# First SwiGLU under the second attention: silu of a token block in one piece, behind all eight first products

## The chip, the cores and the metric

The kernel runs on one core of one Trainium2 chip. The metric is the time of one execution in microseconds (us), as a median over runs; less is better. The engines are TensorE (PE, matmuls and transposes), VectorE (DVE), ScalarE (ACT, activations), GpSimd (POOL) and SyncE (SP, which issues DMAs).

## The reference, cut to what matters

Two transformer layers run over x of 2 batches x 1024 tokens x 256 channels. Layer 0 is windowed self-attention, a cross-attention that keeps the 16 best of 154 keys for each query and head, and a SwiGLU:

```
def _swiglu(h, w_m1, b_m1, w_m2, b_m2):
    u = h @ w_m1 + b_m1                  # 256 -> 2048
    a, b = (u[..., :HID], u[..., HID:])  # HID = 1024
    return jax.nn.silu(a) * b @ w_m2 + b_m2
```

Layer 1 is self-attention over all 1024 tokens, a masked cross-attention and an MLP with gelu. All is float32. Batch 1 still goes through layer 0 while batch 0 is already in layer 1.

## The kernel before, in words

The work of all engines follows one plan. `make_plan` gives every small step a due time by hand, and `Plan.finish` sorts the steps by it. Each engine's program then walks the one sorted list and emits its own part of each step, so that every engine runs its instructions strictly in the plan's order and waits on semaphores for the others. The plan has six stages of projections and MLPs (stage `s`, batch `b`, block `n` of 512 tokens) laid between the steps of four attentions.

The second attention is the one that keeps 16 keys (`topk_run`). A unit of it is one tile of 128 queries for two pairs of heads. Per unit, PE makes the scores of two halves (`c_scores`, L1162) into two of the banks 1 to 4. For each half DVE finds the 16 greatest (`c_top`, L1578 to L1588), ACT negates the maximum (`c_neg`, L1349) and takes the exponential (`c_exp_all`, L1359), and POOL masks it (`c_pick`, L1664 and L1666). PE turns both halves (`c_tail` and `c_turn`, L1173 and L1181) and ACT copies them (`c_copy`, L1370). The scores of a unit may overwrite a bank only when the exponential of the unit two before has read it. Every fourth unit is followed by the product with the values (`c_pv`, L1194 and L1196), a copy by ACT (`o_copy`, L1344) and a transpose (`o_turn`, L993).

Under this attention, two slots to a unit, lies the first SwiGLU for batch 0 (stage 3, `b` = 0, blocks 0 and 1), built by `gap_slots`. For a block, PE makes eight first products `ua` j = 0 to 7 (L1056; two matmuls of 128x512 in the program, four rows in the trace), each into bank 0 or 6, and ACT adds the bias and copies each to `hidden` (`ua_copy`, L1304), which frees the bank. Then come eight second products `ub` (also L1056), each multiplied by DVE with the silu of the first (`hid`, L1533), then the down projection (L1070). The silu runs on `hidden` in place, on ACT, in four instructions q = 0 to 3 of 128x1024 (two products j each, L1320). silu and exp stand in different activation tables: a silu after an exp, and an exp after a silu, is preceded by a table load (ACT_TABLE_LOAD). For batch 0 the plan puts q = 0, 1 behind the copy of j = 3 and q = 2, 3 behind that of j = 7. For batch 1 all four stand behind j = 7. The product `hid` j waits until silu q = j // 2 is done:

```
elif kind == "hid":
    dve.wait_ge(*g.ran("ub", s, b, n, j))
    dve.wait_ge(m.silu_done, plan.n("silu", s, b, n, j // 2) + 1)
```

Each place at which ACT goes over to silu and back is called a break below: block 0 has its first break at 323.2 us and its second at 337.8 us of the trace, block 1 at 429.8 us and 441.6 us.

Of the kernel before, what the change touches and what calls it, by code (L numbers as in the profile page):

```python
# [20 lines left out]
HT = HID // P  # L21
# [280 lines left out]
def gap_slots(s, b, n, apart=0):  # L302

    gap = [[]] * apart
    p0, p1 = 2 * n, 2 * n + 1
    if s in ATTENDED:
        rows = [] if s == 2 or (s, b) == (3, 0) or (s, b, n) == (3, 1, 0) else [("row", s, b, p0, 0), ("row", s, b, p1, 0)]
        head = [rows + [("on_turn", s, b, p0), ("on_copy", s, b, p0), ("on_turn", s, b, p1), ("on_copy", s, b, p1)],
                *gap, [("y_mm", s, b, p0), ("x_sum", s, b, p0), ("stats", s, b, p0)],
                [("y_mm", s, b, p1), ("x_sum", s, b, p1), ("stats", s, b, p1), ("rstd", s, b, n)], *gap]  # L310
    else:
        head = [[("stats", s, b, p0), ("stats", s, b, p1), ("rstd", s, b, n)], *gap]
    turns = [x for k in range(CK) for x in (("hat_turn", s, b, n, k), ("modulate", s, b, n, k))]
    head += [[("x_hat", s, b, p0), ("x_hat", s, b, p1)], *gap, turns]
    if s == 3:
        tail = gap + [[("ua", s, b, n, j), ("ua_copy", s, b, n, j)] for j in range(HT)]
        tail[apart + 2].append(("row", s, b, p0, 1))
        tail[apart + 6].append(("row", s, b, p1, 1))
        for j in ((HT - 1,) if b else (3, HT - 1)):
            tail[j + apart] += [("silu", s, b, n, q) for q in range(j // 4 * 2 * (1 - b), (j + 1) // 2)]  # L320
        tail += [[("ub", s, b, n, j), ("hid", s, b, n, j)] for j in range(HT)]
        for p in (p0, p1):
            tail += [[("down_part", s, b, p, 0)], [("down_part", s, b, p, 1)], [("down_part", s, b, p, 2)], [("down", s, b, p), ("out_sum", s, b, p)]]
        return head, tail
    tail = gap + [[("qk", s, b, n, u), ("qk_a" if s == 2 or u % 2 == 0 else "qk_d", s, b, n, u)] for u in range(UNITS[s])]
    if s in HAS_V:
        for t in (n * 4, n * 4 + 2):
            tail.append([("v", s, b, t), ("v_copy", s, b, t), ("v", s, b, t + 1), ("v_copy", s, b, t + 1)])
    return head, tail
# [188 lines left out]
def make_plan():  # L518
# [13 lines left out]
    plan.spread(mod, T + 0.4 * W, T + 2 * W)  # L532
    between = lambda first, last, per: [T + (c + (0.62 + i) / per) * R for c in range(first, last) for i in range(per)]
    plan.fill(joined([gap_slots(1, 1, n) for n in range(2)]), between(5, 15, 2), (0.2 * R, 0.3 * R))
    plan.at(T + 4.0 * W, ("load_w", "wa1"))
    plan.at(T + 18 * R, *[("row", 2, 0, p, 0) for p in range(4)], *[("row", 2, 1, p, 0) for p in range(4)], ("load_row", 2), ("load_row", 3))
# [8 lines left out]
    ctx.append([("load_vt",)])  # L545
    plan.spread(ctx, T + 3.6 * W, T + 5.2 * W)
    plan.fill(joined([gap_slots(2, 0, n, 1) for n in range(2)]), between(23, 33, 2), (0.2 * R, 0.3 * R))
    step = 5.2
    A2 = end + 3
# [8 lines left out]
    def under(first, last, slots, per, aside=0.3):  # L558
        return plan.fill(slots, [A2 + (first + (i + aside) / per) * step for i in range(int((last - first) * per))], (0.25 * step, 0.9 * step, 0.5 * step))

    under(1, 18, joined([gap_slots(2, 1, n) for n in range(2)]), 1)
    under(1, 7, late, 1, 0.8)
    plan.at(A2 + 8.5 * step, ("stash",), ("load_w", "m1"), ("load_w", "m2a"))
# [1318 lines left out]
```

## Time and profile before

| | before |
|---|---|
| median of 3 runs | 1472.02 us (1468.61 to 1472.67) |
| profiled execution, its own time | 1467.48 us |
| its span, first to last instruction | 1465.7 us |
| PE busy | 1359.6 us, 93% |
| DVE busy | 901.9 us, 62% |
| ACT busy | 726.0 us, 50% |
| POOL busy | 346.1 us, 24% |
| mean granted TensorE clock | 0.972 |

The profile is one execution. Its own time is 1.8 us over its span. A busy share is an average over stages that differ: what a change is worth is read where it lies. In rows of a timeline, the bracket at the end is the time the engine was idle before the row, and what released it.

### The profile page before, as it was taken

The page shows a single profiled execution, that of the slowest core. Times are in us where ns is not written, and L with a number is a line of the kernel's source. Part 1 is how long each engine was busy: PE and PEld are TensorE (multiplying, and loading weights), DVE is VectorE, ACT ScalarE, POOL GpSimd, SP SyncE. Part 2 cuts the span into 40 slices and gives each one's busy share as a digit, 9 for nine tenths or more (in the row PEclk, how much of TensorE's full clock was granted, in tenths as well). Part 3 has the DMA queues.
Part 4 walks back from the last instruction along what each step waited for, and adds up shares of the span by engine and source line. Part 5 has one row for each costly group of instructions (what it writes and reads, how often), then busy time and mean ns, then how long its engine had stood idle before and what let it go on. Part 6 is the DMA issues. An engine that isn't in the chain of part 4 may idle for free.

```text
span 1465.7 us, 25433 instructions
## 1 busy us (share of the span) xinstructions
PE 1359.6 (93%) x9100; PEld 681.3 (46%) x9100; DVE 901.9 (62%) x2785; ACT 726.0 (50%) x1484; POOL 346.1 (24%) x397
## 2 busy tenths in 40 slices
PE   7989887889999888999899999999999989989998
PEld 5457654444644653442233333343333335545676
DVE  3656579988888896765565666666676346640220
ACT  2245456665485564035544565555556664543221
POOL 1013257876666664010000100000010011010220
PEclk9999989889999999999999999999999999999999
DMA  6011003000000000000010000000000000000000
GB/s 196 21 56 34 17 19 107 2 15 1 1 2 12 30 2 28 1 1 1 1 52 21 1 2 0 2 1 1 1 12 1 2 1 2 13 6 0 15 19 29
DMA packets 22093, 26.75 MB, mean 18 GB/s; under 512 B 4204, under 2 KB 19634, under 8 KB 21708
## 3 DMA queue, kind: packets, MB, share of 16 engines
q1 hardware_dynamic: 21059, 25.03, 5.3%
q8 instruction: 73, 1.20, 0.3%
q14 instruction: 52, 0.43, 0.1%
q10 hardware_dynamic: 909, 0.10, 0.1%
HBM read 21.58 MB, written 3.08 MB: 17 GB/s over the span
## 4 chain that ended last, share of the span: by engine, by line
PE 78%; DVE 11%; ACT 4%; issue 4%; POOL 1%; DMA 1%; SPq 0%; ACTq 0%; DVEq 0%; POOLq 0%
PE bank L1098 27%; PE bank L1056 11%; PE bank L1138 8%; PE bank L1070 7%; PE bank L1035 5%; PE bank L1014 4%; PE bank L993 2%; PE bank L1162 2%; PE bank L1041 2%; DVE left L1581 2%; PE bank L1181 1%; DVE x_hat L1526 1%; DVE top L1578 1%; DVE left L1588 1%; PE bank L1021 1%
## 5 line engine op out<-in xcount | busy, mean ns | idle before, releaser
L1337 ACT ACTIVATE pr<-bank 128x512 f32<-128x512 f32 x656 | 353.4, 598 | 283.6 <-PE bank L1098 270.3
L1553 DVE TENSOR_REDUCE part_max<-bank 128x1 f32<-128x512 f32 x512 | 327.2, 685 | 178.5 <-PE bank L1098 178.0
L1098 PE MATMUL bank<-slot 32*128 32x512 f32 (+1 forms) x3072 | 388.2, 522 | 10.8 <-ACT pr L1337 6.1
L1098 PEld LDWEIGHTS bank<-slot 32*128 32x128 f32 x3072 | 162.6, 187 | 209.5 <-issue 157.8
L1605 POOL TENSOR_SCALAR var_eps<-mean_var 128x4 f32<-128x4 f32 x24 | 5.5, 229 | 882.5 <-DVE mean_var L1517 882.0
L1664 POOL TENSOR_SCALAR left<-left 128x308 f32<-128x308 f32 x128 | 125.3, 979 | 76.0 <-issue 34.3
L1138 PE MATMUL bank<-pr,v 128*17 128x512 f32 x1024 | 135.2, 600 | 0.2
L1056 PE MATMUL bank<-h_t,w_m 128*128 128x512 f32 x256 | 127.9, 625 | 4.3 <-DVE o_all L1497 3.2
L1666 POOL TENSOR_TENSOR probs<-left,exp_all 128x308 f32<-128x308 f32 x128 | 107.5, 840 | 10.7
L1359 ACT ACTIVATE exp_all<-bank,neg 128x154 f32<-128x154 f32 x256 | 85.6, 386 | 6.6 <-DVE left L1581 2.1
L1578 DVE MAX8 top<-bank 128x8 f32<-128x154 f32 x256 | 69.5, 313 | 30.6 <-PE bank L1162 30.0
L1557 DVE TENSOR_REDUCE neg_max<-bank 128x3 f32<-128x462 f32 (+1 forms) x96 | 50.7, 579 | 52.1 <-PE bank L1098 51.8
L1581 DVE MATCH_REPLACE8 left<-top,bank 128x154 f32<-128x154 f32 x256 | 76.8, 308 | 0.0
L1588 DVE MATCH_REPLACE8 left<-top,left 128x154 f32<-128x154 f32 x256 | 75.7, 303 | 0.3 <-issue 0.3
L1056 PEld LDWEIGHTS bank<-h_t,w_m 128*128 128x128 f32 x256 | 45.0, 195 | 64.2 <-issue 57.4
L1506 DVE TENSOR_TENSOR x_sb<-x_sb,bank 128x512 f32<-128x512 f32 x32 | 21.9, 684 | 83.6 <-PE bank L1014 83.6
L1344 ACT ACTIVATE o_st<-bank 128x512 f32<-128x512 f32 x64 | 38.3, 599 | 60.9 <-PE bank L1143 30.1
L1584 DVE MAX8 top<-left 128x8 f32<-128x154 f32 x256 | 68.1, 307 | 0.0
L1014 PE MATMUL bank<-w_out,o_norm_t 128*128 128x256 f32 x256 | 64.9, 398 | 1.4 <-DVE x_sb L1506 1.4
L1035 PE MATMUL bank<-h_t,wa 128*128 128x512 f32 x128 | 63.6, 625 | 2.7 <-ACT h_t L1270 2.0
L1636 POOL TENSOR_TENSOR x_sb<-x_sb,res_row 128x512 f32<-128x512 f32 x48 | 60.2, 1274 | 22.9 <-DMA res_row<-rows_dram 15.6
L1550 DVE TENSOR_REDUCE neg_max<-bank 128x4 f32<-128x512 f32 x64 | 40.9, 682 | 39.5 <-PE bank L1098 39.5
(142 smaller groups left out, 1757.0 us busy)
## 6 DMA issues: line engine op xcount, KB each, us to landing
w_m<-in_L_xcond_w_m SPq DMA_DIRECT2D x1, 2048.0 KB, 7.9
w_m<-in_L_xcond_w_m SPq DMA_DIRECT2D x2, 1024.0 KB, 7.9
w<-in_L_xcond_w SPq DMA_DIRECT2D x2, 1024.0 KB, 6.6
w_ada<-in_L_xcond_w_ada SPq DMA_DIRECT2D x1, 1792.0 KB, 10.1
x_sb<-in_x SPq DMA_DIRECT2D x6, 256.0 KB, 6.3
res_row<-rows_dram SPq DMA_DIRECT2D x12, 128.0 KB, 3.4
out_x<-x_sb SPq DMA_DIRECT2D x6, 256.0 KB, 2.1
wa<-in_L_xcond_w_qkv SPq DMA_DIRECT2D x1, 768.0 KB, 6.6
```

Of the source, the lines that this page charges most:

```text
L1014: last = nc.tensor.matmul(bank[:, tt * C:(tt + 1) * C], m.o_norm_t[:, slot, k, tt * P:(tt + 1) * P], m.w_out[:, j % 2, k, :], start=(k == ...
L1035: last = nc.tensor.matmul(bank[:, :], w[:, k, c0:c0 + P], m.h_t[:, slot, k, :], start=(k == 0), stop=(k == CK - 1))
L1056: last = nc.tensor.matmul(bank[:, :], w[:, k, c0:c0 + P], m.h_t[:, slot, k, :], start=(k == 0), stop=(k == CK - 1))
L1070: last = nc.tensor.matmul(bank[:, tt * C:(tt + 1) * C], m.hidden[:, j, t * P:(t + 1) * P], w, start=(j == 0), stop=(j == HT - 1))
L1098: last = nc.tensor.matmul(g.bank(*tile)[:, into], left, right, start=True, stop=True)
L1138: last = nc.tensor.matmul(out[h * HW:h * HW + VE, :], m.v[b][:, d % TB, heads[h], :], m.pr[:, slots[h], :], start=(d % TB == 0), stop=(d % ...
L1337: nc.scalar.activation(m.pr[:, u % NPR, :], g.bank("s", gi, i)[:, :], ACT.Exp).then_inc(g.free("s", gi, i), 1)
L1553: nc.vector.tensor_reduce(m.part_max[:, slot, h * TB + i // 8, i // 4 % 2:i // 4 % 2 + 1], bank[:, :], axis=AX.X, op=ALU.max).then_inc(don ...
L1581: nc.vector.match_replace(m.left1[:, v % 2, hh, :], m.top[:, v % 4, hh, 0:8], bank[:, hh * C:hh * C + S2], -FAR).then_inc(m.left1_done, 1)
L1588: nc.vector.match_replace(m.left2[:, v % 4, hh, :], m.top[:, v % 4, hh, 8:16], m.left1[:, v % 2, hh, :], -FAR).then_inc(m.left2_done, 1)
L1664: nc.gpsimd.tensor_scalar(left, left, -FAR, None, ALU.is_equal).then_inc(m.marked, 1)
L1666: nc.gpsimd.tensor_tensor(m.probs[:, u % 2, 2 * hf:2 * hf + 2, 0:S2], left, m.exp_all[:, v % 4, :, :], ALU.mult).then_inc(m.pick_done, 1)
```

## The change

For batch 0 the four silu instructions of a block stand together behind the copy of the eighth first product, as they did for batch 1 only.

```diff
@@ gap_slots, s == 3
         tail[apart + 6].append(("row", s, b, p1, 1))
-        for j in ((HT - 1,) if b else (3, HT - 1)):
-            tail[j + apart] += [("silu", s, b, n, q) for q in range(j // 4 * 2 * (1 - b), (j + 1) // 2)]
+        tail[HT - 1 + apart] += [("silu", s, b, n, q) for q in range(HT // 2)]
         tail += [[("ub", s, b, n, j), ("hid", s, b, n, j)] for j in range(HT)]
```

The steps of PE, DVE, POOL and SP come in the same order as before. Only ACT's order changes, at four places (two in each of the blocks 0 and 1 of batch 0). The change is one line shorter, so that lines behind it have numbers one lower.

ACT at the first break of block 0, before (L1304 the copies of products, L1320 silu, L1359 exp, L1344 the copy of the attention's values):

```order
L1304 ACTIVATE hidden<-bank,columns 128x512
L1320 ACT_TABLE_LOAD
L1320 ACTIVATE hidden<-hidden 128x1024 x2
L1349 ACTIVATE neg_74<-top 128x2
L1344 ACTIVATE o_st<-bank 128x512
L1359 ACT_TABLE_LOAD
L1359 ACTIVATE exp_all<-bank,neg_74 128x154 x2
L1304 ACTIVATE hidden<-bank,columns 128x512
```

The same place in the change:

```order
L1303 ACTIVATE hidden<-bank,columns 128x512
L1348 ACTIVATE neg_74<-top 128x2
L1343 ACTIVATE o_st<-bank 128x512
L1358 ACTIVATE exp_all<-bank,neg_74 128x154 x2
L1303 ACTIVATE hidden<-bank,columns 128x512
```

Two table loads and two silu instructions are gone from between the copies of the fourth and the fifth product.

ACT at the second break of block 0, before:

```order
L1304 ACTIVATE hidden<-bank,columns 128x512
L1320 ACT_TABLE_LOAD
L1320 ACTIVATE hidden<-hidden 128x1024 x2
L1349 ACTIVATE neg_74<-top 128x2
L1359 ACT_TABLE_LOAD
L1359 ACTIVATE exp_all<-bank,neg_74 128x154 x2
L1370 ACTIVATE probs_t<-bank 128x4x128
```

The same place in the change:

```order
L1303 ACTIVATE hidden<-bank,columns 128x512
L1319 ACT_TABLE_LOAD
L1319 ACTIVATE hidden<-hidden 128x1024 x4
L1348 ACTIVATE neg_74<-top 128x2
L1358 ACT_TABLE_LOAD
L1358 ACTIVATE exp_all<-bank,neg_74 128x154 x2
L1369 ACTIVATE probs_t<-bank 128x4x128
```

The two silu instructions stand here now, as four in a row between the same two table loads. In block 1 the same moves happen.

## Rows read from the trace of the kernel before

**Rows 1.** Page, busy time of each engine (share of the span) and instructions.

```profile
PE 1359.6 (93%) x9100; PEld 681.3 (46%) x9100; DVE 901.9 (62%) x2785; ACT 726.0 (50%) x1484; POOL 346.1 (24%) x397
```

**Rows 2.** Page, chain that ended last, shares of the span by engine.

```profile
PE 78%; DVE 11%; ACT 4%; issue 4%; POOL 1%; DMA 1%; SPq 0%; ACTq 0%; DVEq 0%; POOLq 0%
```

**Rows 3.** Stretches: length, busy of PE, PEld, DVE, ACT, POOL (count), PE clock, DMA.

```profile
343.00:387.00 44.00, 43.70 (x272) 25.87 (x272) 36.19 (x181) 18.95 (x61) 30.70 (x34) 1.00 0.01 2
...
430.00:447.00 17.00, 15.03 (x76) 6.58 (x75) 13.06 (x73) 16.35 (x30) 8.89 (x10) 1.00 0.08 24
```

**Rows 4.** Groups on ACT, forms apart: line, count, busy us, mean ns, idle before.

```profile
L1320 ACT ACTIVATE hidden<-hidden 128x1024 f32<-128x1024 f32 x16 | 15.8, 1046 | 0.1
...
L1320 ACT ACT_TABLE_LOAD x6 | 7.7, 1283 | 0.1
```

**Rows 5.** Timeline of ACT, block 0's first break: start us, length us, what.

```profile
326.53 0.57 ACT L1344 ACTIVATE o_st<-bank 128x512 f32<-128x512 f32 x1
...
328.42 0.67 ACT L1359 ACTIVATE exp_all<-bank,neg 128x154 f32<-128x154 f32 x2
328.98 0.69 ACT L1304 ACTIVATE hidden<-bank,columns 128x512 f32<-128x512 f32 x1
```

**Rows 6.** Timeline of ACT, second breaks: block 1 (first row), block 0 (the others).

```profile
440.84 0.69 ACT L1304 ACTIVATE hidden<-bank,columns 128x512 f32<-128x512 f32 x1 [0.33 <-PE bank L1056]
...
337.04 0.69 ACT L1304 ACTIVATE hidden<-bank,columns 128x512 f32<-128x512 f32 x1 [0.33 <-PE bank L1056]
...
339.04 2.00 ACT L1320 ACTIVATE hidden<-hidden 128x1024 f32<-128x1024 f32 x2
340.95 0.19 ACT L1349 ACTIVATE neg<-top 128x2 f32<-128x2 f32 x1
...
342.45 0.67 ACT L1359 ACTIVATE exp_all<-bank,neg 128x154 f32<-128x154 f32 x2
```

**Rows 7.** Timeline of PE around the four breaks.

```profile
328.10 0.60 PE L993 MATMUL bank<-ident,o_st 128*128 128x128 f32 x4
329.72 1.98 PE L1056 MATMUL bank<-h_t,w_m 128*128 128x512 f32 x4 [1.02 <-ACT hidden L1304]
...
343.27 0.79 PE L1162 MATMUL bank<-kc,slot 32*128 32x154 f32 x8 [0.96 <-ACT exp_all L1359]
...
345.90 0.42 PE L1173 MATMUL bank<-ident,probs 128*32 128x128 f32 x8
...
435.44 0.79 PE L1162 MATMUL bank<-kc,slot 32*128 32x154 f32 x8 [1.07 <-ACT exp_all L1359]
...
447.06 0.79 PE L1162 MATMUL bank<-kc,slot 32*128 32x154 f32 x8 [0.96 <-ACT exp_all L1359]
```

**Rows 8.** Timeline of POOL, the pick that the transposes at 345.90 need.

```profile
344.33 0.84 POOL L1666 TENSOR_TENSOR probs<-left,exp_all 128x308 f32<-128x308 f32 x1
```

**Rows 9.** Timeline of ACT, a batch 1 block with four silu in a row.

```profile
700.20 3.89 ACT L1320 ACTIVATE hidden<-hidden 128x1024 f32<-128x1024 f32 x4
704.11 1.28 ACT L1337 ACT_TABLE_LOAD   x1
```

**Rows 10.** Timeline of PE, first work behind two longer idle times elsewhere.

```profile
306.57 1.16 PE L1021 MATMUL bank<-ident,x_hat 128*128 128x128 f32 x8 [2.54 <-ACT x_hat L1312]
...
549.65 1.63 PE L1021 MATMUL bank<-ident,x_hat 128*128 128x128 f32 x8 [3.25 <-ACT x_hat L1312]
```

**Rows 11.** Stretches of 8 us behind idle times of PE: length, PE busy, PE clock.

```profile
86.83:94.83 8.00, 8.00 (x99) 1.00 0.01 2
...
306.57:314.57 8.00, 8.00 (x40) 0.58 0.01 2
...
549.65:557.65 8.00, 7.37 (x44) 0.79 0.00 1
572.35:580.35 8.00, 8.00 (x29) 1.00 0.00 0
...
343.27:351.27 8.00, 8.00 (x46) 1.00 0.01 2
```

## The prediction

> **What bounds the kernel now.** I read the page first: PE is busy for 93% of the span, ACT for half of it [rows 1], and the chain that ended last lies for 78% on PE and for 4% on ACT [rows 2]. So a piece of ACT work costs time only where PE stands still for it. I then read the stretches around the SwiGLU. In 343 to 387 PE is busy for 43.70 of 44.00 us and ACT for 18.95; in 430 to 447, which holds both breaks of block 1, ACT is busy for 16.35 of 17.00 us and PE for 15.03 [rows 3]. The work between the breaks is PE's, and at the breaks ACT is late. Last I read the timelines of ACT and PE at the four breaks. PE waits once behind each of them, for 1.02 and 0.96 us in block 0 and for 1.07 and 0.96 us in block 1, each time released by ACT [rows 7]. These four waits, 4.01 us together, are all that the present breaks cost, and they are what the change can touch.
>
> **The change part by part.** *Work removed.* Per block two table loads of 1.283 us go [rows 4], so ACT does 4 x 1.283 = 5.1 us less in all. The 16 silu instructions all remain. None of this counts by itself, since ACT is not the bound; what counts is when the copies and exponentials behind the breaks are done.
>
> *First breaks.* In block 0 the silu stand before the copy of the attention's values at 326.53, a table load, the exponential at 328.42 and the copy of the fifth product at 328.98 [rows 5]. PE has nothing more to do from 328.10 + 0.60 = 328.70 on and starts the sixth product at 329.72, in the bank that this copy frees [rows 7]. Without two table loads and 2.00 us of silu before it, some 4.6 us, the copy is done before 328.70 (it needs to come 1.0 us sooner), so the wait goes whole: -1.02. In block 1 the scores at 435.44 wait for an exponential, and that wait goes in the same way: -1.07. Sum -2.09 us.
>
> *Second breaks.* Here ACT arrives with nothing in arrear: it waited 0.33 us for PE before the copy of the eighth product, at 337.04 and at 440.84 [rows 6]. Since it was waiting for PE, the break starts as much sooner as PE does, and not more. The silu take longer: two take 2.00 us and end in the negation at 340.95, 1.91 us after their start [rows 6]; four in a row take from 700.20 to 704.11, 3.91 us [rows 9]. The difference is 2.00 us, and the exponential at 342.45, for which PE's scores at 343.27 wait [rows 6, 7], comes 2.00 us later against the break's start. PE has only the two second products and the transposes to do in between, as before, and had used these up 0.96 us before the exponential came. So the whole 2.00 us is idle time of PE, in each block: +4.00 us. The wait becomes 0.96 + 2.00 = about 2.96 us.
>
> *What is queued behind it.* On ACT the copy of the transposes and two more exponentials stand behind the longer break; all of them serve work that PE reaches only behind the late scores. The next transposes start at 345.90 and need the pick that POOL ends at 344.33 + 0.84 = 345.17 [rows 7, 8]. That pick waits for the same exponential as the scores, so both move by the same amount and the slack of 0.73 us stays. DVE multiplies the first second product when silu q = 0 is done, which is one silu behind the break's start, as soon as it wants it. I cost all of that at nothing. Nor does anything give the delay back: the 44 us behind are PE's own [rows 3]. DMAs, POOL's and SP's queues are not moved past.
>
> Sum without the clock: -2.09 + 4.00 = **+1.91 us**.
>
> *The clock.* The waits of about 1 us leave the granted clock alone: 1.00 over the 8 us from 343.27 on [rows 11]. The trace shows no wait of 2.96 us here, so I bound its price by the nearest rows, PE's idle times between 2.4 and 3.3 us. There are eight that begin at full clock. Behind two of them the clock stayed full, as at 86.83 and 572.35; behind three the mean over 8 us was 0.79 or 0.80, as at 549.65 (idle before it 3.25 us); behind three it was 0.56 to 0.58, as at 306.57 (idle before it 2.54 us) [rows 10, 11]. The clock then stood at its lower level, 1.2 GHz in place of 2.4, for part of the stretch. Time lost is 8 x (1 - clock), where PE is busy throughout: 0, 1.7 or 3.4 us. Behind the new waits PE is busy throughout, so this would be lost in full. Two waits with chances of 2, 3 and 3 in 8 give a sum of 0 (6%), 1.7 (19%), 3.4 (33%), 5.1 (28%) or 6.8 us (14%). I take **3.4 us**, the likeliest.
>
> The Trainium skill ("TensorE: Matmul & The Clock Gate", section "HAM oscillation — how this bites in real kernels") says that waits between pieces of matmul work can throttle the array anew each time, and asks for loops without them. It speaks against this change, which makes one longer wait from two short ones; the rows agree that long waits lower the clock, though not each one does. [...]
>
> **Forecast**: +1.91 + 3.4 = **+5.3 us**. The profiled execution took 1467.48 us, so the sum gives 1472.8 on it. The median shown, 1472.02, is 4.5 us above that execution, which is of the size of what one or two stretches of low clock are worth; on the median the forecast is **1477.3 us**. Some 0.3% of this kernel, 4.4 us, can be told from no change.
>
> **The rivals.**
> *The clock holds at both new waits.* The two idle times after which it did so [rows 11] speak for it, the other six against. Time +1.9, that is 1473.9 us.
>
> *The longer burst is absorbed.* If PE made up the 2.00 us later, because what it waits for later (a DVE sum or a copy) is not moved by the delay, only the gains stay: -2.1, that is 1469.9 us. Against it: the scores are made by PE, and DVE and POOL start from them, so that everything moves with PE.
>
> *ACT is the bound in the blocks, and the kernel gets faster.* At 96% busy in 430 to 447 [rows 3], ACT might set the pace there. Then a block shortens by the work removed, 2 x 1.283 = 2.57 us, two blocks by 5.1: 1466.9 us. This decides if ACT reaches the second break in arrear to PE, from that point on. The 0.33 us that it waited for PE there, in both blocks [rows 6], speak against it.
> The Trainium skill ("ScalarE: Activation LUTs", section "What ACT_TABLE_LOAD costs") adds a drain to each load and puts a switch at about 2.66 us. An estimate from that page gives 4 x 2.66 = 10.6 us saved on ACT, and this rival would lead to 1461.4 us. The trace disagrees: from the end of the negation, 340.95 + 0.19, to the exponential at 342.45 a switch takes 1.31 us [rows 6].
>
> *The change does not do what it says*: the order on ACT shows that it does. I give it nothing.
>
> **How the numbers follow.** The clock falls at one or both new waits, the forecast: 0.70, with times of 3.6 to 8.7 us over the median, 1475.6 to 1480.7. The clock holds: 0.13. Absorbed: 0.10. ACT the bound: 0.04. Something dearer, as a wait that grows behind the burst: 0.03. The range from **1470 to 1482 us** takes in the forecast's whole range, the case of a held clock and most of the absorbed one, and a us more on top for the spread of the runs. Slower by over 0.3% needs +4.4 us: that is the forecast except for its case of one short fall, some 0.53, and the dearer case: **0.55**. Within 0.3%: that one case, the held clock and the absorbed one: **0.39**. Faster by over 0.3%: **0.06**, ACT as bound and a lucky clock.
>
> **What would show it.** Right: ACT has four table loads fewer (two of L1319 in place of four for batch 0) and is busy some 5 us less; no wait of PE for ACT at the sixth product of block 0 nor at the scores behind the fourth product of block 1; one wait of 2.8 to 3.1 us before the scores at each second break, released by the exponential; up to two new stretches of low clock right behind them. The first step is wrong if PE still waits at the first breaks, the second if the waits at the second breaks are under 2.5 us or PE's idle time shrinks later by as much. The forecast as a whole is wrong if the waits are as said and the clock stays full behind both, or if lower clock elsewhere in the trace, at waits that the change does not touch, moves by more than this.

## The result and the profile after

The change makes the kernel 0.33% slower: the ratio to the kernel before is 1.0033, with a 95% interval of 1.0021 to 1.0046, that is 4.9 us (3.1 to 6.8) on 1470. The median is 1474.18 us over 20 runs, that of the kernel before 1469.98 us, also over 20 runs; these medians lie 4.2 us apart, which is inside the interval. The three runs known ahead lay 2 us higher. One of the 20 runs of the change was disturbed (2166.39 us at a mean clock of 0.555) and is left out of the ratio and of all that follows; the median without it is 1474.07 us.

| | after |
|---|---|
| median | 1474.18 us |
| profiled execution, its own time | 1470.45 us |
| its span | 1468.7 us |
| mean granted TensorE clock | 0.974 |

The profiled execution is the third fastest of the 20, and only 3.0 us slower than that of the kernel before.

The page of the change, busy time of each engine, against [rows 1]:

```profile
PE 1358.5 (92%) x9100; PEld 680.2 (46%) x9100; DVE 901.3 (61%) x2785; ACT 721.3 (49%) x1480; POOL 346.0 (24%) x397
```

ACT has four instructions fewer and is busy 4.7 us less, and the kernel is slower all the same. The groups of ACT say what went (line, count, busy us, mean ns, idle before), against [rows 4]; the loads before an exponential are two fewer as well:

```profile
L1319 ACT ACTIVATE hidden<-hidden 128x1024 f32<-128x1024 f32 x16 | 15.6, 1044 | 0.0
L1319 ACT ACT_TABLE_LOAD x4 | 5.1, 1283 | 0.1
...
L1358 ACT ACT_TABLE_LOAD x2 | 2.6, 1283 | 0.0
```

The timeline of PE after, block 0, then block 1, against [rows 7]:

```profile
306.04 1.16 PE L1020 MATMUL bank<-ident,x_hat 128*128 128x128 f32 x8 [2.54 <-ACT x_hat L1311]
...
326.46 0.42 PE L1172 MATMUL bank<-ident,probs 128*32 128x128 f32 x8
326.82 0.66 PE L1180 MATMUL bank<-ident,probs 128*128 128x128 f32 x4
327.31 0.60 PE L992 MATMUL bank<-ident,o_st 128*128 128x128 f32 x4
327.75 1.88 PE L1055 MATMUL bank<-h_t,w_m 128*128 128x512 f32 x4
329.56 0.79 PE L1161 MATMUL bank<-kc,slot 32*128 32x154 f32 x8
...
338.35 1.88 PE L1055 MATMUL bank<-h_t,w_m 128*128 128x512 f32 x4
343.08 0.79 PE L1161 MATMUL bank<-kc,slot 32*128 32x154 f32 x8 [2.86 <-ACT exp_all L1358]
343.81 2.70 PE L1055 MATMUL bank<-h_t,w_m 128*128 128x512 f32 x4
...
387.14 0.79 PE L1161 MATMUL bank<-kc,slot 32*128 32x154 f32 x8
...
411.65 1.22 PE L1020 MATMUL bank<-ident,x_hat 128*128 128x128 f32 x8 [0.78 <-ACT x_hat L1311]
...
433.86 0.79 PE L1161 MATMUL bank<-kc,slot 32*128 32x154 f32 x8
...
447.38 1.39 PE L1161 MATMUL bank<-kc,slot 32*128 32x154 f32 x8 [2.86 <-ACT exp_all L1358]
448.71 2.07 PE L1193 MATMUL bank<-tails_t,vt 128*128 128x512 f32 x2
...
495.15 0.79 PE L1161 MATMUL bank<-kc,slot 32*128 32x154 f32 x8
```

Four rows of PE before, which [rows 7] does not have and to which these are compared below:

```profile
331.63 0.79 PE L1162 MATMUL bank<-kc,slot 32*128 32x154 f32 x8
...
386.02 0.79 PE L1162 MATMUL bank<-kc,slot 32*128 32x154 f32 x8
...
412.09 1.22 PE L1021 MATMUL bank<-ident,x_hat 128*128 128x128 f32 x8 [0.78 <-ACT x_hat L1312]
...
491.80 0.79 PE L1162 MATMUL bank<-kc,slot 32*128 32x154 f32 x8
```

The waits at the first breaks are gone: the sixth product follows the transposes at 327.75 without one, and so do block 1's scores at 433.86. At each second break PE now stands still for 2.86 us where it was 0.96 us. Behind it rows take longer than the same work before: the product at 343.81 takes 2.70 us in place of 1.99, the scores at 447.38 take 1.39 us in place of 0.79.

The timeline of ACT after at the second break of block 0, against [rows 6]:

```profile
334.97 0.69 ACT L1303 ACTIVATE hidden<-bank,columns 128x512 f32<-128x512 f32 x1 [0.33 <-PE bank L1055]
335.67 1.28 ACT L1319 ACT_TABLE_LOAD   x1
336.97 3.90 ACT L1319 ACTIVATE hidden<-hidden 128x1024 f32<-128x1024 f32 x4
340.77 0.19 ACT L1348 ACTIVATE neg<-top 128x2 f32<-128x2 f32 x1
340.98 1.28 ACT L1358 ACT_TABLE_LOAD   x1
342.27 0.67 ACT L1358 ACTIVATE exp_all<-bank,neg 128x154 f32<-128x154 f32 x2
```

ACT waits the same 0.33 us for PE before the break as it did before, so it had no arrears there to win back. From the start of the copy at 334.97 to the exponential at 342.27 it is 7.30 us; before it was 5.41 us, from 337.04 to 342.45.

Stretches of 8 us after, from the first work behind five waits of PE (length, PE busy, PE clock), against [rows 11]:

```profile
343.08:351.08 8.00, 8.00 (x37) 0.79 0.01 2
447.38:455.38 8.00, 8.00 (x26) 0.58 0.00 0
306.04:314.04 8.00, 8.00 (x40) 0.58 0.01 2
390.76:398.76 8.00, 8.00 (x50) 0.79 0.00 0
504.62:512.62 8.00, 7.74 (x44) 0.79 0.00 1
```

The first two are the new waits: the clock fell behind both, worth 1.7 and 3.4 us by the prediction's 8 x (1 - clock). The rows give it directly, since the same work follows in both traces: from the late scores to the last scores shown of each block it is 42.75 us before (343.27 to 386.02) and 44.06 after (343.08 to 387.14), and 44.74 us (447.06 to 491.80) against 47.77 (447.38 to 495.15) in block 1. So the low clock cost 1.31 and 3.03 us, 4.3 us in this execution, and none of it came back in the 43 to 45 us behind. At two waits that the change does not touch it fell for less long than before (0.79 where the kernel before shows 0.57, at 389.64 and at 501.26). By the mean clock, this execution spent 76 us in all at the lower level, the one of the kernel before 82 us, the new stretches included. Such differences come and go from run to run, so one execution does not show what the clock costs on the mean.

**Where the time went.** Laid side by side, the two traces give the part that comes from the waits. I measure from PE's transposes of x_hat (at 306.57 and 412.09 before, 306.04 and 411.65 after) to the late scores:

| | before | after | difference |
|---|---|---|---|
| block 0, to the scores behind the sixth product | 25.06 | 23.52 | -1.54 |
| block 0, from there to the late scores | 11.64 | 13.52 | +1.88 |
| block 1, to the scores behind the sixth product | 23.35 | 22.21 | -1.14 |
| block 1, from there to the late scores | 11.62 | 13.52 | +1.90 |
| sum | | | +1.10 |

The part that differs from run to run is read from the mean granted clock that every run lists: 2 x span x (1 - clock) is the time that a run spent at the lower level, and at most half of it is lost, where PE is the bound and its work takes twice as long. Before it is 85.0 us on the mean (31 runs taken beside the experiments, standard error 1.2), after 92.0 us (19 runs, 2.3): 7.0 us more at the lower clock (standard error 2.6), and at most 3.5 us lost. The runs themselves give less than half: inside the 31 runs of before, and inside the 19 of the change, each us more at the lower clock went with 0.37 us more of time (standard error 0.04 in both). By that the 7.0 us are an estimated 2.6 us. So the sum is 1.1 + 2.6 to 3.5 = 3.7 to 4.6 us, against 4.9 (3.1 to 6.8) measured. The chip of the change's 20 runs is not on record; the kernel before shows 85.0 us on one chip and 85.2 us on another.

### The profile page after: what moved, and what is told of

The parts are those of the page before. It is cut to its first block, busy times and chain, and to the rows that moved or that the text cites. A ratio compares the mean times of both kernels' runs of the same rounds, so it can differ in the third digit from the quotient of the medians.

```text
span 1468.7 us, 25429 instructions
## 1 busy us (share of the span) xinstructions
PE 1358.5 (92%) x9100; PEld 680.2 (46%) x9100; DVE 901.3 (61%) x2785; ACT 721.3 (49%) x1480; POOL 346.0 (24%) x397
## 4 chain that ended last, share of the span: by engine, by line
PE 80%; DVE 10%; ACT 3%; issue 3%; POOL 1%; DMA 1%; SPq 0%; ACTq 0%; DVEq 0%; POOLq 0%
PE bank L1097 27%; PE bank L1055 12%; PE bank L1137 8%; PE bank L1069 7%; PE bank L1034 5%; PE bank L1013 4%; PE bank L1161 2%; PE bank L992 2%; PE bank L1180 2%; PE bank L1040 2%; PE bank L1020 1%; DVE left L1580 1%; DVE x_hat L1525 1%; DVE top L1577 1%; DVE left L1587 1%
```

## The experiments

All times below are against runs of the kernel before on the same chip, with the ratio's interval. Half-clock time is the figure just explained, the mean time of a run at the lower clock. The four runs up to the exponential ahead of the burst share one chip, the last two another.

**First breaks taken out.**

```diff
-            nc.scalar.activation(both, both, ACT.Silu).then_inc(m.silu_done, 1)
+            if b == 0 and q < 2:
+                nc.scalar.activation(m.pad_s[:, 2 * n + q:2 * n + q + 1], m.marks[:, 0:1], ACT.Copy).then_inc(m.silu_done, 1)
+            else:
+                nc.scalar.activation(both, both, ACT.Silu).then_inc(m.silu_done, 1)
```

> The kernel before, with the first two silu of both blocks of batch 0 left out (a copy of one column in their place, so that the first breaks and their four table loads are gone and the second breaks are as before). My account, from the two traces laid side by side: the first breaks cost 1.5 us in block 0 and 1.15 us in block 1, so the kernel is 2.6 us faster than before, about 1467.4 us, and PE's waits at the second breaks stay at 0.96 us each. Rival A, the cost is only the idle time that the profile names before the waiting instruction: 2.1 us faster. Rival B, ScalarE's work is the bound in the blocks: four silu (4 us) and four loads (5.1 us) less, so 9 us faster.

Measured: 1463.76 us, ratio 0.9966 (0.9950 to 0.9981), 5.0 us faster (2.8 to 7.4). The waits at the second breaks stayed as they were:

```profile
339.75 0.79 PE L1163 MATMUL bank<-kc,slot 32*128 32x154 f32 x8 [0.96 <-ACT exp_all L1363]
...
440.85 0.79 PE L1163 MATMUL bank<-kc,slot 32*128 32x154 f32 x8 [0.96 <-ACT exp_all L1363]
```

From the transposes of x_hat (at 304.54 and 407.00) to these scores it is 35.21 and 33.85 us, 1.49 and 1.12 us less than before: the 2.6 us of my account are there, and rival A's 2.1 falls short of them. But the total gained more than that. The half-clock time fell from 85.0 to 74.4 us (standard errors 1.2 and 2.0), which is worth 3.9 us at 0.37 us each and 5.3 us at most. Rival B, 9 us, lies outside the interval, and its mechanism is not in the trace. My number was a miss: it left the clock out.

**Second breaks made longer.** The first breaks stay; two more silu go to a scratch tile at each second one.

```diff
             nc.scalar.activation(both, both, ACT.Silu).then_inc(m.silu_done, 1)
+            if b == 0 and q == 3:
+                for i in range(2):
+                    nc.scalar.activation(m.burn[:, :], m.m1[:, 0, 0:1024], ACT.Silu).then_inc(m.burned, 1)
+                    act.wait_ge(m.burned, 2 * n + i + 1)
```

> The kernel before, with two more silu of 128x1024 into a scratch tile at each second break of batch 0, the first breaks left as they are: the dear half of the change alone. My account: PE's wait at each second break grows by some 2 us to about 3.0 us, which is 3.8 to 4.2 us in all, and low clock behind one or both adds 1.7 to 6.8 us, on the mean 3.4: 7.4 us slower than before, 1477.4 us, with new stretches of low clock right behind the second breaks in the profile. Rival C, the clock has no part in it: 4 us slower, clock full behind the breaks. Rival D, the longer burst is absorbed: under 1 us slower.

Measured: 1476.93 us, ratio 1.0054 (1.0032 to 1.0076), 7.9 us slower (4.7 to 11.2). Half-clock time 93.0 us. The timeline of PE at the two second breaks, then the 8 us behind each, in the profiled execution, which was the slowest of the eight (1484.29 us):

```profile
352.77 1.40 PE L1164 MATMUL bank<-kc,slot 32*128 32x154 f32 x8 [3.14 <-ACT exp_all L1365]
...
459.85 0.79 PE L1164 MATMUL bank<-kc,slot 32*128 32x154 f32 x8 [3.14 <-ACT exp_all L1365]
```

```profile
352.77:360.77 8.00, 8.00 (x28) 0.62 0.00 0
...
459.85:467.85 8.00, 7.91 (x39) 0.79 0.00 0
```

Both waits grew to 3.14 us (the two added silu took 2.13 us), and the clock fell behind both. From the work before the break to the late scores it is 2.17 and 2.18 us more than before; with 8.0 us more at the lower clock (standard error 2.9), 3.0 to 4.0 us lost, that makes 7.3 to 8.3. Rival C's 4 us lies below the interval, rival D's 1 us far below.

**The long wait filled.** The change, with the second of the second products made twice in both blocks.

```diff
-            for k in range(CK):
-                last = nc.tensor.matmul(bank[:, :], w[:, k, c0:c0 + P], m.h_t[:, slot, k, :], start=(k == 0), stop=(k == CK - 1))
+            for _ in range(2 if kind == "ub" and (b, j) == (0, 1) else 1):
+                for k in range(CK):
+                    last = nc.tensor.matmul(bank[:, :], w[:, k, c0:c0 + P], m.h_t[:, slot, k, :], start=(k == 0), stop=(k == CK - 1))
```

> The change, with the second of the eight second products of both blocks of batch 0 made twice in the same bank (same result), so that PE works 1.9 us of each long wait away and stands still for about 1.0 us only. My account: the time at which the exponential comes is the same, so the 1.1 us of delay stay, but the clock no longer falls behind the waits: 1.1 us slower than before, some 3 to 3.5 us faster than the change, clock 1.00 over the 8 us behind both waits. Rival C, the clock has no part in it: as slow as the change, 4.2 us over before. Rival E, PE's added work delays what follows: slower than the change by up to 3.8 us.

Measured: 1470.67 us, ratio 1.0003 (0.9983 to 1.0024), 0.4 us slower than before (2.5 faster to 3.5 slower), though PE does 3.8 us more work than in the change; I had said 1.1 us slower. The timeline of PE and the 8 us behind:

```profile
343.05 0.79 PE L1162 MATMUL bank<-kc,slot 32*128 32x154 f32 x8 [1.14 <-ACT exp_all L1359]
...
447.46 0.79 PE L1162 MATMUL bank<-kc,slot 32*128 32x154 f32 x8 [1.14 <-ACT exp_all L1359]
```

```profile
343.05:351.05 8.00, 7.99 (x46) 1.00 0.01 2
...
447.46:455.46 8.00, 7.91 (x44) 1.00 0.01 2
```

The late scores come when they do in the change (37.10 and 35.73 us behind the transposes at 305.95 and 411.73, the change 37.04 and 35.73), but the clock stays full behind both, and half-clock time is 82.3 us (standard error 2.6) against the change's 92.0. In this trace the work behind the late scores takes as long as before, 42.76 us (343.05 to 385.81) and 44.74 us (447.46 to 492.20), without the 1.31 and 3.03 us of the change. This is the run that tells the clock's part from the wait's: rivals C and E both ask for 4 us or more over the kernel before, and the interval ends at 3.5.

**The exponential ahead of the burst.** One burst of four per block, as in the change, but due later, so that on ACT the exponential which the scores wait for comes first.

```diff
 def fill(self, slots, times, later=(0.0, 0.0)):
...
-                self.at(time + (later[2] if ...
+                self.at(time + (0.38 * 5.2 if step[0] == "silu" and step[2] == 0 else 0.0) + (later[2] if ...
```

> The change, with the four silu of batch 0 due 0.38 of a unit later, so that on ScalarE the exponential for which PE's scores wait comes ahead of the table load, and the burst behind it. My account: in block 0 the scores no longer wait; what waits are the transposes and later scores, by 0.5 us or less, so block 0 is 1.9 us faster than before; in block 1 the product with the values needs a copy that stands behind the burst, so PE waits some 2.0 us there and the block is even with before. Together 2 us faster than before, 1468 us, if the wait of 2.0 us leaves the clock alone, and 0 to 1.4 us slower than that if not. Rival F, any burst of four costs the same wherever it stands: as slow as the change.

Measured: 1464.39 us, ratio 0.9968 (0.9949 to 0.9988), 4.7 us faster than before (1.8 to 7.5) with the same table loads as in the change. Half-clock time is 79.1 us (standard error 2.7). The timeline of ACT at the second break of block 0, and of PE in the same place and in block 1:

```profile
335.18 0.67 ACT L1358 ACTIVATE exp_all<-bank,neg 128x154 f32<-128x154 f32 x2
335.87 1.28 ACT L1319 ACT_TABLE_LOAD   x1
337.16 3.90 ACT L1319 ACTIVATE hidden<-hidden 128x1024 f32<-128x1024 f32 x4
340.96 0.57 ACT L1369 ACTIVATE probs_t<-bank 128x512 f32<-128x512 f32 x1
```

```profile
339.56 0.79 PE L1161 MATMUL bank<-kc,slot 32*128 32x154 f32 x8
...
345.15 0.79 PE L1161 MATMUL bank<-kc,slot 32*128 32x154 f32 x8
...
442.16 1.13 PE L1193 MATMUL bank<-tails_t,vt 128*128 128x512 f32 x2 [1.73 <-ACT probs_t L1369]
```

In block 0 the burst, four silu and two table loads or 6.5 us, costs PE nothing: the scores at 339.56 and those at 345.15 start without a wait. In block 1 the product with the values waits 1.73 us for a copy behind the burst, where I had said 2.0, and the clock fell behind it (0.79 over 8 us). Rival F falls. My number, 2 us, was low again, though inside the interval: to the product with the values block 1 is 0.5 us shorter than before (35.32 us from the transposes of x_hat at 406.84, 35.86 before), to the scores at 345.15 block 0 is 2.5 us shorter (39.76 from 305.39 on, against 42.26), and the 5.9 us less at the lower clock are some 2 us more.

**Two bursts in block 1, both behind an exponential.** The silu are due 0.38 of a unit later, as in the run just told, and the second pair of block 1 one whole unit (5.2 in the plan) more:

```diff
+def silu_later(step):
+    return 5.2 * (1.38 if step[3] == 1 and step[4] > 1 else 0.38)
```

> As the run with the exponential ahead of the burst, but in block 1 the four silu are split again: two behind the exponential at the eighth first product, two one unit later, also behind an exponential, where ScalarE has little to do (19 of 44 us busy in that stretch of the kernel before). My account: the 1.73 us wait of PE before the product with the values in block 1 goes, and no new one comes; against the kernel before all four waits are gone, 1.49 + 1.12 us at the first breaks and 0.97 us at each second one, 4.5 us, plus what fewer stretches of low clock give: 5 to 7 us faster, about 1464 us, with ScalarE's busy time 2.6 us above that of the change. Rival B, table loads are what costs: slower than the run with one burst per block by 2.6 us.

Measured: 1461.45 us, ratio 0.9945 (0.9926 to 0.9964), 8.1 us faster than before (5.3 to 10.9), and some 13 us better than the change, each against its own runs of before. Half-clock time is 74.0 us, but from six runs only (standard error 5.3). The timeline of PE in block 1:

```profile
439.36 0.79 PE L1166 MATMUL bank<-kc,slot 32*128 32x154 f32 x8
440.08 1.12 PE L1198 MATMUL bank<-tails_t,vt 128*128 128x512 f32 x2
...
447.14 0.79 PE L1166 MATMUL bank<-kc,slot 32*128 32x154 f32 x8
```

No wait is left in it. ACT is busy for 723.5 us, 2.2 us more than in the change, and the kernel is faster: rival B falls, the number of table loads does not decide. The range I gave, 5 to 7 us, ended just short of the measured value, within its interval. How much of the 8.1 us is the four waits and how much the clock, six runs do not tell.

**More work, no other waits.** The kernel before, with the sixth second product of block 0 made twice.

```diff
+            for _ in range(2 if kind == "ub" and (b, n, j) == (0, 0, 5) else 1):
```

> The kernel before, with the sixth second product of block 0 of batch 0 made twice (same result): 1.9 us more work for PE at a place where PE is the bound and the breaks are over, so that no wait changes and only the distance from the waits ahead to the waits behind grows. Expected if low clock comes by chance alone: 1.9 us slower than before, half-clock time per run unchanged at about 85 us. Rival G, whether a wait lowers the clock hangs on its distance from earlier waits: the half-clock time per run moves by 5 us or more either way, and the total by some 2 us beside the 1.9.

Measured: 1469.79 us, ratio 0.9998 (0.9981 to 1.0015), from 2.8 us faster to 2.2 us slower. The 1.9 us of added work lie inside this interval too. Half-clock time is 79.3 us against 85.2 (standard errors 2.5 and 1.3). This is 5.9 us less, as rival G has it, but only some two standard errors; it points to G and does not settle it.

## Why the prediction was right

The forecast was slower by 5.3 us; measured are 4.9 (3.1 to 6.8). The median of 1474.2 us lies 3 us under the predicted 1477.3, of which 2 us are the base: the three runs of before lay above the 20 that came later. On the profiled executions it is 3.0 us against 5.3, for the reason told under the rivals below. All terms came out with the right sign, the two that are read from the traces within 0.6 us; that the total came so near is in part luck, since the clock's term alone has a standard error of some 1 us.

*First breaks.* Given -2.09 us, the sum of the idle times that the profile names; measured -1.54 and -1.14, together -2.68, and 2.61 with the breaks taken out alone. The mechanism was right and the size was low. In block 0 the transposes at 327.25 started 2.12 us after the product before them, and start 1.91 us after it now: they need the value bank, which the copy of the attention's values (L1344) frees, and that copy stood behind the silu. I had not followed this wait, since it is too short to be listed. Another 0.16 us is that the listed idle time starts at the modelled end of the transposes (328.10 + 0.60), while without a wait the next product starts 0.44 us behind their start: from one start to the other it is 1.62 us before and 0.44 after. And 0.1 us is that work flows closer when PE does not stop: the sixth product takes 1.98 us behind its wait [rows 7] and 1.88 us without one. So the four listed waits were not all that the breaks cost. A slip of counting stands in the prediction too: the scores at 435.44 are behind the sixth product of block 1, not the fourth.

*Second breaks.* Given +4.00, measured +3.78. The wait is 2.86 us, given as 2.96. Cause: I took the four silu from a place where a table load follows, which starts at their end [rows 9]; here the negation follows, and starts 3.80 us behind their start, as it starts 1.91 us behind that of two [rows 6]. Two more silu so cost 1.89 us and not 2.00.

*Nothing queued behind, nothing given back.* Held: transposes, picks and products move with the scores.

*The clock.* Given 3.4 us as the likeliest of 0 to 6.8; the runs show 2.6 to 3.5 on the mean. In the profiled execution it fell behind both waits and cost 4.3 us there; 8 x (1 - clock), the prediction's price, gives 5.1 and is somewhat high. The rows show one reason: not all of the work takes twice as long at the lower clock (the scores 1.39 us against 0.79). That the clock matters was shown, not only argued: with the same delay but PE kept at work, the stretches behind the waits are as short as before and half-clock time went back to that of before. The size on the mean is less sure. The prediction gave the first breaks no part in the clock. Yet with only these taken out half-clock time fell by 10.6 us, with only the second breaks made longer it rose by 8.0 us, and the change, which has both, shows 7.0 us more and not 2.6 less (the sum's standard error is near 4). And the change with its waits filled and the kernel without first breaks both wait only some 1 us at these places and still differ by 8 us (82.3 and 74.4).

*The rivals.* The held clock (+1.9) lies under the measured interval. The absorbed burst fell by the second experiment. ACT as the bound fell by the page itself: 4.7 us less ACT work and a slower kernel. The prediction named lower clock at waits that the change does not touch as a way to be wrong. In the profiled pair this did happen: outside the new stretches the execution of the change spent some 16 us less at the lower clock than the one of before, more than the 10 us that the new waits brought, and so that pair lies 3.0 us apart and not 5.4. On the mean over the runs it did not: the 7.0 us more are near the 7.7 us that the prediction's chances give for two such waits. Of its chances, that of slower by over 0.3% is a little low by its own numbers: 0.70 without the case of one short fall (a fifth of it) is 0.56, and not 0.53.

## What to carry to other kernels

Where an activation has to change tables inside another engine's stream, count table loads last: ask first which result the bound engine waits for next, and put the burst behind it. Here one burst of four silu costs 1.9 us of new wait when it stands ahead of one exponential. Behind it it costs nothing in block 0, and 1.73 us of wait in block 1, where a copy that PE needed stood behind the burst in its turn. And price a longer wait of the matmul engine above its length: in the traces here its clock stayed full behind the breaks' waits of about 1 us and fell behind those of 1.73, 2.86 and 3.14 us, which by the sum above made up some two thirds to three quarters of what this change cost. It is a chance and not a rule: behind two of the eight waits of 2.4 to 3.3 us in the kernel before it stayed full.

## What the runs showed that I had not expected

The stretches of low clock elsewhere in the kernel are not a fixed cost. With only the first breaks removed, waits of about 1 us behind which the profile shows a full clock, half-clock time fell by 10.6 us per run (85.0 to 74.4), and the total gained 5.0 us (2.8 to 7.4), about twice the waits. Either short waits lower the clock in some executions, or the distance between waits that remain decides whether the clock falls behind them; the run with more work points to the second, and neither is settled. For a change of a few us this is as large as the change: the waits that it moves have to be counted, and the clock of many runs read beside them.
